# A graph layer's dense part: one-hots of the low digit on ScalarE, four tiles behind a group, a fourth part of ten groups, the matrix laid out block by block, and the tile check in another PSUM bank

## What is computed

```python
def _gcn_conv(x, src, dst, ew, W, b, n_nodes):
    xW = x @ W
    deg = jax.ops.segment_sum(ew, dst, num_segments=n_nodes) + 1.0
    dinv = jnp.where(deg > 0, jax.lax.rsqrt(deg), 0.0)
    norm = dinv[src] * ew * dinv[dst]
    agg = jax.ops.segment_sum(norm[:, None] * xW[src], dst, num_segments=n_nodes)
    agg = agg + (dinv * dinv)[:, None] * xW
    return agg + b
...
x = x + gnn(layernorm(x))     # relu(conv1), relu(conv2), 256 -> 256 -> 256
x = x + moe(layernorm(x))     # router, top 2 of 8 experts, gelu(t @ w1 + b1) @ w2 + b2
```

## Time and profile before

| | |
|---|---|
| Median of three runs | 4186.57 us (4186.05 to 4193.72) |
| The profiled execution's own time | 4192.1 us |
| Its span, first to last instruction | 4190.3 us |
| Busy in the span | PE 91%, PEld 84%, DVE 70%, POOL 67%, ACT 19% |
| Before layer 1 | 0 to 233.5 us |
| Layer 1, first to last gather | 233.5 to 1976.1 us |
| From the last gather of layer 1 to the first of layer 2 | 17.0 us |
| Layer 2 | 1993.1 to 4190 us |

### The profile page before, as it was taken

How to read it: one execution, slowest core, us unless ns; L and a number is a source line. 1 busy time by engine, 2 the same in 40 slices (tenths; PEclk the granted TensorE clock), 3 DMA queues, 4 the chain that set the end, 5 groups by cost and what they waited for, 6 DMA issues and landing times.

```text
span 4190.3 us, 80198 instructions
## 1 busy us (share of the span) xinstructions
PE 3805.6 (91%) x26207; PEld 3509.1 (84%) x26208; DVE 2934.6 (70%) x10218; ACT 816.7 (19%) x2532; POOL 2790.4 (67%) x2930
## 2 busy tenths in 40 slices
PE   7768888888888888977899999999999999999999
PEld 7557777777777786866799999999999999999999
DVE  6667828855555537232688888888888888888887
ACT  4410100100000000000122222222222222222222
POOL 3157767776667667676777666666766676666663
PEclk9989999999999999977899999999999999999999
DMA  6243453354444453553443333333333333333332
GB/s 155 83 124 114 119 155 112 114 146 123 139 124 143 127 153 115 153 152 100 121 116 110 109 109 110 106 109 109 109 106 109 109 109 106 109 109 109 106 109 58
DMA packets 273302, 492.68 MB, mean 118 GB/s; under 512 B 61086, under 2 KB 179937, under 8 KB 272884
## 3 DMA queue, kind: packets, MB, share of 16 engines
q0 software_dynamic: 137664, 376.10, 32.0%
q1 hardware_dynamic: 126906, 105.30, 8.2%
q10 hardware_dynamic: 8314, 6.06, 0.6%
HBM read 448.55 MB, written 38.67 MB: 116 GB/s over the span
## 4 chain that ended last, share of the span: by engine, by line
PE 71%; POOL 9%; DVE 8%; issue 6%; DMA 4%; ACT 1%; DVEq 1%; SPq 0%; POOLq 0%; ACTq 0%
PE part L978 20%; PE psH L963 17%; PE psY L972 17%; POOL msg L588 8%; PE psY L1044 6%; PE psH L978 3%; PE psY L1036 3%; PE psG L928 2%; DMA work<-ytab 2%; DVE wbuf L1584 2%; DVE sel L1377 1%; DMA ytab<-msg 1%; DVE wbuf L1578 1%; DVE wbuf L1577 1%; PE psG L909 1%
## 5 line engine op out<-in xcount | busy, mean ns | idle before, releaser
L588 POOL DMA_INDIRECT msg<-ytab,srcT x2868 | 2740.9, 956 | 1252.6 <-issue 776.7
L978 PE MATMUL part<-sel,msg 128*128 128x96 f32 x8880 | 1124.9, 282 | 68.3 <-DMA msg<-ytab,srcT 68.1
L978 PEld LDWEIGHTS part<-sel,msg 128*128 128x128 f32 x8880 | 1107.3, 201 | 84.8 <-DMA msg<-ytab,srcT 39.8
L963 PEld LDWEIGHTS psH<-work,wbuf 128*128 128x128 f32 x6272 | 808.1, 192 | 35.4
L972 PE MATMUL psY<-wbuf,work 128*128 128x256 f32 x3136 | 822.2, 385 | 0.0
L963 PE MATMUL psH<-work,wbuf 128*128 128x128 f32 x6272 | 810.8, 275 | 0.0
L725 ACT ACTIVATE work<-psH,b_s 128x128 f32<-128x128 f32 x1568 | 491.2, 364 | 1406.8 <-PE psH L963 1406.8
L1377 DVE TENSOR_SCALAR sel<-iota,relT,ewT 128x96 f32<-128x96 f32 x2868 | 752.9, 339 | 1.9 <-ACT accbuf L670 1.2
L1386 DVE TENSOR_TENSOR accbuf<-accbuf,part 128x192 f32 x555 | 194.8, 351 | 545.0 <-PE part L978 544.5
L972 PEld LDWEIGHTS psY<-wbuf,work 128*128 128x128 f32 x3136 | 535.7, 191 | 40.6 <-ACT work L725 0.3
L1036 PE MATMUL psY<-wbuf 128*128 128x196 f32 x1072 | 286.9, 372 | 112.1 <-DVE wbuf L1584 75.8
(11 more groups left out here) (249 smaller groups left out, 2799.0 us busy)
## 6 DMA issues: line engine op xcount, KB each, us to landing
msg<-ytab,srcT POOLq DMA_INDIRECT x2868
work<-ytab SPq DMA_DIRECT2D x294, 128.0 KB, 2.8
ytab<-xS SPq DMA_DIRECT2D x99, 128.0 KB, 3.5
ytab<-msg SPq DMA_DIRECT2D x98, 128.0 KB, 1.9
xS<-in_x SPq DMA_DIRECT2D x98, 128.0 KB, 2.5
out<-resb SPq DMA_DIRECT2D x98, 128.0 KB, 1.9
...
```

Of the source, the lines that this page charges most:

```text
L588: pool.indirect_dma_start(msg[:, r * GT + j, :], None, ytab[l], bass.IndirectOffsetOnAxis(ap=srcT[:, g * GT + j:g * GT + j + 1].bitcast(U3 ...
L963: mm = pe.matmul(psH[e % 2][:, m * P:(m + 1) * P], w1_s[:, e, k, m * P:(m + 1) * P], tokS[s.u][:, k, :], start=(k == 0), stop=(k == KD - 1))
L978: m = pe.matmul(slot[:, h * W:(h + 1) * W], msg[:, tile0 + j, h * P:(h + 1) * P], sel[:, sel0 + j, :], start=(j == 0), stop=(j == GT - 1))
```

## The change

What is different, by its parts. Line numbers in the pieces of order below are of each kernel's own file: L836 and L865 are the window step's matmuls, L844 and L874 the first check matmul, L848 and L878 the second, L978 and L1008 the products, L1036 and L1068 the outers.

- **Low digit on ACT.** The one-hot of the low digit is no longer made on DVE (L1577). ACT makes it in two activations of 128x128, |iota - low| and then relu(1 - that), with eight buffers instead of four. ACT makes them in its slot loop: those for the second group of a slot behind `sums`, those for the groups from the third to the next slot's first behind `back`. PE waits for both halves (`s_hot`, `s_low`).
- **Four tiles behind a group** instead of three; the part's tiles have widths `WTS` = (3,4,4,5) nodes instead of 4, so the second one-hot, the outer product and the add have 147, 196, 196 and 245 columns.
- **A fourth part of ten groups.** 77 groups are dense (308 tiles), 315 are gathered (1,260 DMAs instead of 1,300). Tiles stand behind groups 4 to 42, 59 to 97, 114 to 129, 146 to 161, 178 to 189, 206 to 217, 234 to 243 and 260 to 269, blocks behind the 13 groups after each: 154 tile groups instead of 180, 104 block groups instead of 78. 75 slots are three groups long. The last slot of layer 1 has two groups, and the experts' weights are loaded from slot 90 instead of 88.
- **Matrix nodes side by side.** `mat` is laid out block by block: a dense matmul reads 128 neighbouring columns. The add of a tile now writes 49 runs of 3, 4 or 5 neighbours, 128 words apart.
- **Check in its own bank.** `ps_first` and `ps_out` move from `psT` to `part[0]`, the first bank of the window steps. PE's first check matmul goes from behind step 10 to behind step 22 and waits until ACT has copied that bank out (`s_win` at 1); the DVE check goes from step 35 to step 29, is done part by part, and waits for the router's transposes alone (`s_rwt` at 1), not for ACT's copies; the second matmul goes to behind step 34, and DVE reads its result after step 39.

```diff
-DENSE = (39,16,12)
+DENSE = (39,16,12,10)
-WT = 4
+WTS = (3,4,4,5)
+WT = max(WTS)
+LOWS = 8
-FINAL = 1
+FINAL = 2
-TILES = 3
+TILES = 4
-EARLY, AT_SLOT = 2, 87
+EARLY, AT_SLOT = 3, 89
...
-    ps_first, ps_out = psT[:, 64:64 + ND], psT[0:1, 64 + ND:64 + ND + P]
+    ps_first, ps_out = part[0][:, 0:ND], part[0][0:1, 384:384 + P]
... (ScalarE)
+        def lows(n):
+            tiles = [b for b, at_n in enumerate(TILE_AT) if at_n == n]
+            for b in tiles:
+                wait(act, s_outer, b - LOWS + 1)
+                act.activation(low_s[b % LOWS], iota[:, :], ACT.Abs, bias=low_t[:, TILE[b][2]:TILE[b][2] + 1]).then_inc(s_apart, 1)
+            for b in tiles:
+                act.wait_ge(s_apart, b + 1)
+                act.activation(low_s[b % LOWS], low_s[b % LOWS], ACT.Relu, scale=-1.0, bias=iota[:, 1:2]).then_inc(s_low, 1)
...
                 act.wait_ge(s_added, CUM[min(k, NI)])
                 sums(0, s)
+            if k < NI:
+                lows(CUM[k] + 1)
             if last:
                 back(last, min(k, NS1))
+            if k < NI:
+                for n in range(CUM[k] + 2, CUM[k + 1] + 1):
+                    lows(n)
... (TensorE)
+            if c == 0:
+                pe.wait_ge(s_past, 3)
...
-            if t == SB:
+            if t == 2 * SB + 2:
                 pe.wait_ge(s_edges, 1)
                 pe.wait_ge(s_edgeC, 1)
+                pe.wait_ge(s_win, 1)
                 pe.matmul(ps_first, first_edge, relT[:, 0:ND], start=True, stop=True).then_inc(s_ends, 1)
-            if t == NS - 2:
+            if t == 2 * SB + 14:
...
-            if t == 3 * SB:
+            if t == 2 * SB + 6:
                 pe.wait_ge(s_wts, 6 * 16)
...
             pe.wait_ge(s_hot, b + 1)
+            pe.wait_ge(s_low, b + 1)
             wait(pe, s_mat, b - 1)
-            pe.matmul(psY[b % 2][:, 0:KW], low_s[b % HOT], key_s[b % HOT], start=True, stop=True).then_inc(s_outer, 1)
+            n = WTS[TILE[b][0]] * HB
+            pe.matmul(psY[b % 2][:, 0:n], low_s[b % LOWS], key_s[b % HOT][:, 0:n], start=True, stop=True).then_inc(s_outer, 1)
...
-                m = pe.matmul(psY[k][:, 0:DW], rows_in[j % TB][:, k * P:(k + 1) * P], mat[:, b:b + (DW - 1) * HB + 1:HB],
+                m = pe.matmul(psY[k][:, 0:DW], rows_in[j % TB][:, k * P:(k + 1) * P], mat[:, b * DW:(b + 1) * DW],
... (VectorE)
-            if t == 3 * SB + GC + 1:
+            if t == 2 * SB + 9:
                 v.wait_ge(s_ends, 1)
-                v.wait_ge(s_rwt, 3)
+                v.wait_ge(s_rwt, 1)
                 link(v.tensor_tensor(past, relT[:, 0:ND], ps_first, ALU.subtract))
-                v.tensor_reduce(out_of[:, 0:1], past, axis=AX.X, op=ALU.max)
-                link(v.tensor_reduce(out_of[:, 1:2], past, axis=AX.X, op=ALU.min))
+                for p in range(PH):
+                    tiles = past[:, FIRST[p] * GT:FIRST[p + 1] * GT]
+                    v.tensor_reduce(out_of[:, p:p + 1], tiles, axis=AX.X, op=ALU.max)
+                    link(v.tensor_reduce(out_of[:, PH + p:PH + p + 1], tiles, axis=AX.X, op=ALU.min))
+                    v.tensor_scalar(out_of[:, p:p + 1], out_of[:, p:p + 1], float(WTS[p] - 1), None, ALU.is_gt)
...
+            if t == 3 * SB + GC + 5:
+                v.wait_ge(s_past, 2)
+                v.tensor_reduce(worst[:, :], ps_out, axis=AX.X, op=ALU.max).then_inc(s_past, 1)
...
             wait(v, s_outer, b - HOT + 1)
-            v.tensor_scalar(low_s[b % HOT], iota[:, :], low_t[:, t:t + 1], None, ALU.is_equal)
-            v.tensor_scalar(key_s[b % HOT], iota_k, key_t[c][:, t:t + 1], ewT[:, t:t + 1], ALU.is_equal, ALU.mult).then_inc(s_hot, 1)
+            v.tensor_scalar(key_s[b % HOT][:, 0:n], iota_k[:, 0:n], key_t[c][:, t:t + 1], ewT[:, t:t + 1],
+                            ALU.is_equal, ALU.mult).then_inc(s_hot, 1)
...
-            to = mat[:, bass.ds(place, KW)]
-            v.tensor_tensor(to, to, psY[b % 2][:, 0:KW], ALU.add).then_inc(s_mat, 1)
+            to = mat_nodes[:, :, bass.ds(place, width)]
+            v.tensor_tensor(to, to, psY[b % 2][:, 0:width * HB].rearrange("p (h d) -> p h d", d=width), ALU.add).then_inc(s_mat, 1)
```

53 lines of the change are left out of this document (37 added, 16 removed).

## The result

The changed kernel takes 4171.25 us (median of 16 runs, 4152.81 to 4181.64) beside 4188.25 us of the kernel before (16 runs, 4183.74 to 4196.59): a ratio of 0.9957, 95% interval 0.9947 to 0.9966. It is faster, by 17 us, where 138.6 us were forecast, and its runs lie further apart than those of before. The profiled execution took 4172.2 us (span 4170.4), that of before 4192.1.

A forecast was written before the change was run, and what follows sets the result against it. Layer 1 was taken as bound by POOL's gathers (1.2585 us each) plus stalls for PE: 1585.7 + 20 = 1606 against 1742.6 us; with -2 us in front, 4186.6 - 138.6 = 4048 us, range 4022 to 4105.

The forecast's parts named there:

- Before layer 1: Front: DVE's 15.44 us wait at the check goes, PE waits about 10 us for ACT's copy; sum -2 us, between -5 and +6.
- POOL's own work: Layer 1's gathers: 40 fewer at 1.2585 us each, -50.3 us; 1,260 take 1585.7 us.
- Layout, price of a matmul: Dense matmul on PE: neighbouring columns take 129 ns a record instead of 245, 1.85 us less a block group.
- Block groups and gaps: PE's runs of thirteen block groups: 68 us instead of 92, 77 with the gap, under POOL's 80.5; eight give back 28 us.
- The wait for rows once a slot stays: Block groups: each slot's first block still waits for rows loaded after the store, 49.0 us in all before the change.
- Tile groups: PE's rounds with four tiles: 5.2 us in part 0, 5.5 in parts 1 and 2, 5.8 in part 3; 830 us.
- Stalls: POOL's waits for PE in layer 1: 20 us (13 to 27) instead of 106.5, after PE falls behind by about 27.
- The step was not what made L1044 slow: Rival, dense matmul: `start`/`stop` pattern or banks make it slow, 104 block groups keep 1.85 us each; 4212 us, chance 0.04.
- broken runs at full price: Rival, adds to `mat`: read and write pay 0.3, 0.4, 0.5 us for the three widths; 4236 us, chance 0.03.
- The chain in tile groups is longer: Rival, tile groups: DVE and ACT in PE's loop cost 0.3 us more over 154 groups, 46 us; 4094 us, chance 0.17.
- POOL alone: Rival, layer 1: PE's rounds come out at 5.0, backlog never grows and stalls vanish; 4028 us, chance 0.13.
- The signs named at the end: New profile: gathers about 1606 us, dense matmul 129 to 140 ns; wrong if adds 0.6 us or rows late every group.

The follow-up runs named there:

- E14: The changed kernel with rows asked for ahead of the y2 store, matrix cleared behind PE, check without the wait, first part four wide: 4021.63 us, ratio 0.9597.
- E4: The changed kernel with the matrix laid out as before, a node's words 49 apart: 4252.79 us, ratio 1.0155.
- E1: The changed kernel with the rows of a slot's first block group asked for ahead of the y2 store: 4059.11 us, ratio 0.9682.
- E2: The changed kernel with the matrix cleared in pieces behind PE instead of whole after each sum: 4114.76 us, ratio 0.9824.
- E13: The changed kernel with the first part's products four columns wide per node instead of three: 4157.01 us, ratio 0.9918.
- E10: The changed kernel without the fourth part and with three tiles behind a group instead of four: 4081.94 us, ratio 0.9742.
- E8: The changed kernel without the fourth part, four tiles behind a group kept: 4190.47 us, ratio 1.0001.
- E12: The changed kernel with three edits: rows asked for ahead of the y2 store, matrix cleared behind PE, tiles' check without the wait: 4036.14 us, ratio 0.9637.

## Why the prediction was wrong, step by step

- **Before layer 1** (-2 us forecast, -5.0 measured). The wait that I added was there, and two microseconds shorter than my 10.5, since ScalarE copied the bank at 82.87 us and not at 85.28. Timeline of the changed kernel, answering to the earlier trace rows: that copy, PE's wait, and the first and last instruction of the check on DVE, 2.9 us for a forecast 2.8. The first gather comes at 227.6 to 231.3 us in the six traces with this front, so the 3 us of difference are hardly more than the scatter.

```profile
82.87 0.55 ACT L660 ACTIVATE wbuf<-part 64x480 f32<-64x480 f32 x1
...
83.57 1.37 PE L874 MATMUL part<-relT,accbuf 128*128 128x308 f32 x2 [8.57 <-ACT wbuf L660]
...
95.06 0.47 DVE L1341 TENSOR_TENSOR resb<-relT,part 128x308 f32<-128x308 f32 x1
...
97.84 0.15 DVE L1349 COPY out_of<-out_of 128x1 f32<-128x1 f32 x1
```

- **POOL's own work** (-50.3): right. E14 has 5.034 us a group.
- **Layout, price of a matmul** (245 to 129 ns): the mechanism was right (E4). The size was 154 ns in the change and 135 in E1; the difference is time at the low clock behind late rows.
- **Block groups and gaps, the step that failed.** I put a run of thirteen at 68 us on PE and its gap at 8.7, together under POOL's 80.5, "28 us given back". The trace of the changed kernel, cut in the same way (a tile run begins with its first products, 1.92 us ahead of its first outer, a block run with the last outer, a gap with the last dense matmul):

| PE, us | forecast | measured |
|---|---|---|
| 154 tile groups | 830 | 848.8 |
| eight runs of blocks | 544 (68 each) | 608.4 (76.1 each) |
| seven gaps | 61 (8.7 each) | 103.2 (14.7 each) |
| sum | 1435 | 1560.4 |

That is 90.8 us a cycle and not 76.7: not 28 us given back but 82 more behind, over eight cycles. Two terms were mis-sized. "The wait for rows once a slot stays" treated as a constant what was a moment: the rows come at a fixed time behind the store, so PE, quicker in each group, waits longer for them, 92.9 us in 60 times for 49.0 in 29, and behind the waits its clock is low. Of the 8.1 us a run over the forecast, 3.4 are the wait (11.6 for 8.2) and 4.8 the matmuls at 154 ns instead of 129. E1 takes both away, has 61.6 us a run by the same cut, and lands 11 us from where I had put the kernel. And the gap of "about 2.9 us" a group left out DVE's clear of 5.29 us, for which PE stands; E2 takes the clear out of the gap and leaves 9.0 us. The change has two such gaps more. The 92 us for a run of before were right: 91.3 by the same cut.
- **Tile groups** (830 us on PE forecast, 848.8 measured). The first part took 5.6 us a group instead of 5.2, of which E13 puts some 0.2 down to the clock; parts 1 and 2 took 5.4 instead of 5.5, part 3 5.6 instead of 5.8. Adds were 0.32, 0.37 and 0.41 us, and broken runs cost 0.015 us and less, under the 0.05 taken. ScalarE's waits ahead of `table2` rose by 20.7 us; for a forecast 1.2 in slots of three they are 0.68 on average and 1.1 in 22 slots of tile groups:

```profile
634.47 1.13 PE L958 MATMUL psG<-gw,work 128*128 128x256 f32 x4 [1.11 <-ACT work L701]
```

- **Stalls** (20 us forecast, 147.4 measured). The sum "55 behind, 28 given back, 13 covered by buffers" had the right form, and its terms failed: with the measured ones it is 74 + 82 - 13 = 143 us, and layer 1 took 142.8 more than its gathers' own 1585.7 (the 147.4 come from POOL's waits, with 0.30 us taken off each). The 55 us behind stood in the forecast; what I did not see is how much hung on the runs of blocks giving time back, since a tile group of four tiles, over 5.03 us, never does. In E10 it is the other way round: by the same sum 180 tile groups of three give back 66 us, six cycles of 94.0 us on PE take 81, and of the 15 that are left POOL stood for 6.8. E8 to E10 price the fourth tile at 108 and 116 us.
- **Tail** (unchanged): 15.52 us instead of 16.98.
- **The rivals.** "The step was not what made L1044 slow" and "broken runs at full price" fell (E4). The price of the second was also worked out wrongly: its adds sum to 223 us and not 219, and the 753 ns of L1170 are the mean of 0.51, 0.86 and 0.90 us for one and the same kind of read, so an element that stands alone cost between 0.4 and 1.4 ns there. "The chain in tile groups is longer" gave 4094 us by 0.3 us more in each tile group; it was 0.12 (18.8 / 154), a small part of what was missed. "POOL alone", 4028 us, is where E12 and E14 got to (4036 and 4022), by edits that were no part of the change. The signs named at the end were partly the right ones: rows that come late were listed, for every group though, and once a slot was enough.

The profiled executions differ by 19.9 us (4192.1 and 4172.2) where 138.6 were forecast, 118.7 apart. Layer 1 makes 122.5 of them (1728.5 for 1606), layer 2 0.7, and the front and the tail take 3.0 and 1.5 back. Of the 140 us of stall in the table E1 alone takes away 107, E2 alone 49, and three tiles 103 of E8's 110. They overlap, and no split into shares is claimed.
